# Second self attention: the values due are issued between the third and the fourth score of a step, and the maxima at its end

## The chip, the cores and the metric

The kernel runs on one core of one Trainium2 chip. The metric is the device time of one execution in microseconds, from launch to end. Engines are named as the profile names them: PE is TensorE, PEld its weight loads, ACT ScalarE, DVE VectorE, POOL GpSimd, SP the queue that issues most DMAs.

## The reference

Eight blocks follow one another on x (2 x 1024 tokens of 256): four of attention and four of feed-forward. The change is in the fourth, `_L1_ffn_ref`, whose first half is a self attention with 16 heads of width 16 over 1024 tokens:

```python
h = _layernorm(x, ln1_g, ln1_b)
qkv = h @ w_qkv + b_qkv
q, k, v = jnp.split(qkv, 3, axis=-1)
scores = jnp.einsum('bqhd,bkhd->bhqk', q, k) / np.sqrt(DK)
attn = jax.nn.softmax(scores, axis=-1)
o = jnp.einsum('bhqk,bkhd->bqhd', attn, v).reshape(B, S, D)
x = x + o @ w_o + b_o
```

A projection, a second layer norm and a mixture of experts follow. Everything outside this attention is the same in both kernels.

## The kernel before

The attention is `quad_attention` (stage `heads1`). It takes the 32 pairs of batch and head in 8 groups of four heads. A group has 16 steps: for each half of the 1024 queries (512 wide) and each of the 8 chunks of 128 keys, one step computes the transposed scores of four heads. That makes 128 steps, t = 0 to 127. Each engine has its own hand-written program, and semaphores join them.

What TensorE issues, all from these helpers:

- `score(t, r)` (L1660): one matmul, 66 x 128 weights, 512 columns, for head r. It writes `score_ps`, a ring of 3 buffers, so score number i waits until exponential number i - 3 is done. With four scores a step, the fourth waits for the first exponential of its own step.
- `share(item)` with a peak item (L1638): two bf16 matmuls on 32 rows each, from which VectorE takes part of the row maxima that a later group needs. The two of one item and the two of the next lie on four different strips of rows. They write `shared_ps`, which has two buffers: item number n waits until item n - 2 has been read.
- `value(t)` (L1669): the probabilities of step t times the values, four heads side by side in the columns of the array, 8 matmul records. It waits for the four exponentials of step t, and, for the first chunk of a half (t a multiple of 8), until ScalarE has copied the sums of the half before out of `sums_ps`, the only such buffer.
- `share` with a TURN item (L1643): once a group, the transpose of the group's maxima. `share` with a FOLD item (L1647): once a group, eight transposes of the finished sums. Both use `shared_ps` too, and both stand behind the step's peak items in the table `work_at`.

`work_at[t]` gives a step its items. Items 0 to 39 of 256 peaks are issued ahead of step 0, then two a step, so steps 0 to 107 have two peaks each and steps 108 to 127 none. TURN is in steps 12, 28, ..., 108, FOLD in steps 18, 34, ..., 114 and after the last step.

ScalarE runs the exponentials (L1705) in order. In steps 9, 17, ..., 121 it copies the sums (L1697) after the second exponential. VectorE takes the items in the order of the table: one reduction per peak item (L1721), the minus maxima (L1725), the rows of maxima (L1732, L1734), and for FOLD a reciprocal and a product (L1744, L1748). SP loads the operands of a group, and the rows of maxima after each TURN.

Before the change a step on TensorE is: four scores, the two peaks, the values of the step before, then TURN or FOLD if there is one.

Of the kernel before, what the change touches and what calls it, by code (L numbers as in the profile page):

```python
# [1528 lines left out]
QUAD = 4  # L1529


def quad_attention(nc, core, name, q_dram, k_dram, values, q_narrow, k_narrow, out):
# [39 lines left out]
    with Stage(nc, name) as st:  # L1572
# [52 lines left out]
        def _(pe):  # L1625
# [25 lines left out]
            def score(t, r):  # L1651
                g, half, c = t // PER, t % PER // BT, t % BT
                u = g % 2
                if t % PER == 0 and r == 0:
                    pe.wait_ge(loaded[u], 16 * LOADS * (g // 2 + 1))
                    pe.wait_ge(max_loaded[u], 32 * (g // 2 + 1))
                i = QUAD * t + r
                if i >= RING:
                    pe.wait_ge(exp_done, i - RING + 1)
                pe.matmul(score_ps[:, i % RING, :], k[:, u, r, c * P:(c + 1) * P],  # L1660
                          q[:, u, r, half * 512:(half + 1) * 512], start=True, stop=True).then_inc(score_done, 1)

            def value(t):
                g, c = t // PER, t % BT
                pe.wait_ge(exp_done, QUAD * (t + 1))
                if c == 0 and t:
                    pe.wait_ge(sums_copied, t // BT)
                for r, n in enumerate(heads_of(g)):
                    done = pe.matmul(sums_ps[r * SIDE:(r + 1) * SIDE, :], values[:, n, c, :],  # L1669
                                     probs[:, t % SLOTS_OF_PROBS, r, :], start=(c == 0), stop=(c == BT - 1),  # L1670
                                     tile_position=(0, r * SIDE))
                done.then_inc(value_done, 1)
# [3 lines left out]
                share(item)  # L1676
            for t in range(STEPS):
                items = work_at[t]
                for r in range(QUAD):
                    score(t, r)  # L1680
                for item in items[0:2]:
                    share(item)
                if t:
                    value(t - 1)
                for item in items[2:]:
                    share(item)
            value(STEPS - 1)
            for item in work_at[STEPS]:
# [23 lines left out]
        def _(dve):  # L1712
            def take(item):
                used = number[item]
                two = shared_ps[:, used % 2, :, :]
                dve.wait_ge(shared_done, used + 1)
                if item[0] == PEAK:
                    _, g, s, x, pair = item
                    if g >= 2 and (s, x, pair) == (0, 0, 0):
                        dve.wait_ge(minus_ready, g - 1)  # L1720
# [1328 lines left out]
```

## Time and profile before

| | |
|---|---|
| median of 3 runs | 3163.11 us (3160.62 to 3172.48) |
| the profiled execution | 3165.68 us, its span 3163.9 us |
| mean granted TensorE clock in it | 0.852 of 2.4 GHz |
| PE busy | 2409.5 us (76%) |
| DVE busy | 1544.5 us (49%) |
| ACT busy | 1126.9 us (36%) |
| the 128 steps in the trace | from 1375.8 us to about 1781.5 us |

The span goes from the first to the last instruction. The stages of the program hardly overlap, so a stage is read by itself, as a stretch of the span. PE's busy time counts a matmul from its start until its results are out; matmuls overlap, so it can be 100% while the array isn't. The granted clock is given as a share of 2.4 GHz: 1.00 is 2.4 and 0.50 is 1.2 GHz. In a timeline a row stands for one or more like instructions, with the start of the first, the time to the end of the last, and their number after the x.

### The profile page before, as it was taken

The numbers are of one execution on the slowest core, as the hardware profiler recorded it, in microseconds if no ns is written. First come the engines' busy times: TensorE is split into PE (matmuls) and PEld (weight loads), VectorE is DVE, ScalarE is ACT, GpSimd is POOL, SyncE is SP. The second block draws the span as 40 slices with busy tenths as digits, with TensorE's granted clock in tenths as the row PEclk, the third lists the DMA queues.
The fourth block names the chain that finished last, engine by engine and source line by source line (L and its number), as shares of the span: only waits on it lengthen the run. The fifth ranks groups of instructions, "written<-read, shape, count | busy, mean of one in ns | idle before, by whom it ended". The sixth has DMA issues, their size and how long they took to land. (4 is left out here: it accounts for less than half of the span.)

```text
span 3163.9 us, 38714 instructions
## 1 busy us (share of the span) xinstructions
PE 2409.5 (76%) x12273; PEld 1401.1 (44%) x12274; DVE 1544.5 (49%) x2425; ACT 1126.9 (36%) x2389; POOL 347.7 (11%) x369
## 2 busy tenths in 40 slices
PE   4959999998227587679999729996865999484487
PEld 2413333335117444323333319995333999331254
DVE  4657777763652354667786150002344000347665
ACT  3403333333103235126667424442432444233211
POOL 0010000001004201300000002221001222102211
PEclk9969999999558788759999959998786999686599
DMA  1220010100106300613342146663024666200001
GB/s 55 90 64 22 22 32 21 25 7 11 53 0 203 96 1 19 141 13 45 37 55 28 37 136 213 198 199 124 16 89 144 197 200 198 84 1 28 7 13 33
DMA packets 156570, 233.95 MB, mean 74 GB/s; under 512 B 48758, under 2 KB 110770, under 8 KB 156450
## 3 DMA queue, kind: packets, MB, share of 16 engines
q1 hardware_dynamic: 146754, 205.91, 23.8%
q0 software_dynamic: 9696, 26.49, 2.2%
q8 instruction: 69, 1.13, 0.2%
q14 instruction: 51, 0.42, 0.0%
HBM read 186.56 MB, written 38.86 MB: 71 GB/s over the span
## 5 line engine op out<-in xcount | busy, mean ns | idle before, releaser
L1721 DVE TENSOR_REDUCE heads_part_max<-heads_shared_ps 128x2 f32<-128x1024 f32 x256 | 300.0, 1220 | 90.1 <-PE heads_shared_ps L1638 90.1
L2759 PE MATMUL experts_up_ps<-experts_rowT,experts_w 128*128 128x128 f32 x2864 | 341.0, 277 | 0.0
L1705 ACT ACTIVATE heads_probs<-heads_score_ps 128x512 f32<-128x512 f32 x512 | 266.4, 602 | 191.0 <-PE heads_score_ps L1660 191.0
L2759 PEld LDWEIGHTS experts_up_ps<-experts_rowT,experts_w 128*128 128x128 f32 x2864 | 333.0, 194 | 0.2
L1408 ACT ACTIVATE heads_probs<-heads_score_ps 128x512 f32<-128x512 f32 (+1 forms) x288 | 171.9, 598 | 382.1 <-PE heads_score_ps L1332 380.3
L2909 DVE TENSOR_TENSOR experts_y<-experts_down_ps,experts_b_now 128x256 f32<-128x256 f32 x78 | 33.1, 425 | 555.6 <-PE experts_down_ps L2769 555.6
L1332 PE MATMUL heads_score_ps<-heads_q,heads_k 128*128 128x512 f32 (+1 forms) x576 | 291.6, 616 | 0.3 <-DVE heads_minus_max L1420 0.3
L2819 ACT ACTIVATE experts_hT<-experts_up_ps,experts_b_now 128x128 f32<-128x128 f32 x624 | 222.6, 368 | 46.5 <-PE experts_up_ps L2759 9.8
L1660 PE MATMUL heads_score_ps<-heads_q,heads_k 66*128 66x512 f32 x512 | 198.0, 474 | 29.5 <-ACT heads_probs L1705 25.3
L1420 DVE TENSOR_REDUCE heads_minus_max<-heads_shared_ps 128x1 f32<-128x1101 f32 x120 | 155.9, 1299 | 113.5 <-PE heads_shared_ps L1307 113.4
L2769 PE MATMUL experts_down_ps<-moe_w,experts_hT 128*128 x808 | 184.4, 379 | 0.0
L1660 PEld LDWEIGHTS heads_score_ps<-heads_q,heads_k 66*128 66x128 f32 x512 | 92.2, 201 | 198.4 <-ACT heads_probs L1705 163.5
L2769 PEld LDWEIGHTS experts_down_ps<-moe_w,experts_hT 128*128 128x128 f32 x808 | 148.9, 190 | 17.8
L1344 PE MATMUL heads_sums_ps<-heads_probs,heads_head_values 128*64 128x512 f32 (+1 forms) x576 | 154.6, 605 | 0.0
L1669 PE MATMUL heads_sums_ps<-heads_probs,self_values 128*32 128x512 f32 x1024 | 146.8, 647 | 4.1 <-ACT heads_sums L1697 4.1
L2708 POOL DMA_INDIRECT y_dram<-experts_y,experts_index x101 | 99.4, 985 | 454.3 <-DVE experts_y L2909 410.4
L2769 PE MATMUL experts_down_ps<-l1f_w,experts_hT 128*128 x624 | 141.0, 379 | 0.0
L1458 DVE TENSOR_TENSOR heads_weights<-heads_probs,heads_weights 128x1024 f32<-128x1024 f32 (+1 forms) x112 | 136.2, 1216 | 6.4 <-ACT heads_probs L1408 5.2
L1332 PEld LDWEIGHTS heads_score_ps<-heads_q,heads_k 128*128 128x128 f32 (+1 forms) x576 | 92.1, 187 | 92.4 <-issue 71.5
L2800 ACT ACTIVATE experts_rowT<-experts_rowT_ps 128x256 f32<-128x256 f32 x62 | 23.8, 384 | 296.4 <-PE experts_rowT_ps L2749 296.3
L2769 PEld LDWEIGHTS experts_down_ps<-l1f_w,experts_hT 128*128 128x128 f32 x624 | 115.7, 190 | 14.1
L1307 PE MATMUL heads_shared_ps<-heads_k_peak,heads_q_peak 128*128 128x512 bf16 x360 | 80.9, 335 | 40.7 <-DVE heads_k_peak L1480 26.0
(556 smaller groups left out, 3370.3 us busy)
## 6 DMA issues: line engine op xcount, KB each, us to landing
experts_w<-in_L_ffn_W SPq DMA_DIRECT2D x39, 1024.0 KB, 5.2
experts_w<-in_L_ffn_w SPq DMA_DIRECT2D x39, 1024.0 KB, 5.1
heads_q<-l_queries SPq DMA_DIRECT2D x48, 256.0 KB, 12.1
experts_w<-in_L_ffn_W SPq DMA_DIRECT2D x23, 512.0 KB, 3.9
core_xT<-y_dram SPq DMA_DIRECT2D x20, 512.0 KB, 4.7
experts_b_now<-in_L_ffn_b SPq DMA_DIRECT2D x78, 128.0 KB, 2.9
heads_k<-l_keys SPq DMA_DIRECT2D x32, 256.0 KB, 14.0
l1f_w<-in_L_ffn_W SPq DMA_DIRECT2D x8, 1024.0 KB, 11.9
```

The costliest lines, as they stand in the source:

```text
L1332: pe.matmul(score_ps[0:rows, i % RING, :], k[:, u, c * P:c * P + rows], q[:, u, x:x + spec.unit], start=True, stop=True).then_inc(score_do ...
L1344: done = pe.matmul(sums_ps[x * SIDE:(x + 1) * SIDE, part * spec.unit:(part + 1) * spec.unit], head_values[0:rows, u, c, :], probs[0:rows, ...
L1408: act.activation(probs[0:rows, slot(u, i), :], score_ps[0:rows, i % RING, :], ACT.Exp, scale=spec.scale).then_inc(exp_done, 1)
L1420: dve.tensor_reduce(minus_max[:, u, s:s + 1], src[:, 0:KEYS], AX.X, ALU.max, negate=True).then_inc(shared_read, 1)
L1458: dve.tensor_tensor(total, chunk_probs(u, c)[0:rows, :], chunk_probs(u, 0) if c == 1 else total, ALU.add).then_inc(added, 1)
L1660: pe.matmul(score_ps[:, i % RING, :], k[:, u, r, c * P:(c + 1) * P], q[:, u, r, half * 512:(half + 1) * 512], start=True, stop=True).then_ ...
L1669: done = pe.matmul(sums_ps[r * SIDE:(r + 1) * SIDE, :], values[:, n, c, :], probs[:, t % SLOTS_OF_PROBS, r, :], start=(c == 0), stop=(c == ...
L1705: act.activation(probs[:, t % SLOTS_OF_PROBS, r, :], score_ps[:, i % RING, :], ACT.Exp, scale=SC).then_inc(exp_done, 1)
L1721: dve.tensor_reduce(part_max[:, g % 2, 2 * pair:2 * pair + 2, s, x], two, AX.X, ALU.max).then_inc(shared_read, 1)
L2759: done = pe.matmul(up_ps[:, f % 4, 0:SLOT], w1_sb[:, u, c, f * P:(f + 1) * P], rowT[:, u % 2, c, :], start=(c == 0), stop=(c == DC - 1))
L2769: done = pe.matmul(down_ps[:, u % 2, 0:D], hT[:, u % 2, f, :], second.sb[:, bass.ds(e, 1), f, :].rearrange("p o d -> p (o d)"), start=(f = ...
L2819: act.activation(hT[:, u % 2, f, :], up_ps[:, f % 4, 0:SLOT], func, bias=bias).then_inc(act_done, 1)
```

## The change

In every step TensorE now issues three scores, then the values of the step before, then the fourth score, and then all items of the step: the two peaks, and TURN or FOLD behind them. No instruction is added or removed, and no other engine's program changes.

```diff
@@ -1676,13 +1676,12 @@
                 share(item)
             for t in range(STEPS):
                 items = work_at[t]
-                for r in range(QUAD):
+                for r in range(QUAD - 1):
                     score(t, r)
-                for item in items[0:2]:
-                    share(item)
                 if t:
                     value(t - 1)
-                for item in items[2:]:
+                score(t, QUAD - 1)
+                for item in items:
                     share(item)
             value(STEPS - 1)
             for item in work_at[STEPS]:
```

On PE around the first TURN (steps 12 and 13; L1660 scores, L1638 peaks, L1669 values, L1643 the TURN transpose), before:

```order
L1660 MATMUL heads_score_ps<-heads_q,heads_k 128x512 x4
L1638 MATMUL heads_shared_ps<-self_k_narrow,self_q_narrow 128x512 x4
L1669 MATMUL heads_sums_ps<-heads_probs,self_values 32x512 x4
L1643 MATMUL heads_shared_ps<-core_ident,heads_minus_max 32x128
L1660 MATMUL heads_score_ps<-heads_q,heads_k 128x512 x4
```

and now:

```order
L1660 MATMUL heads_score_ps<-heads_q,heads_k 128x512 x3
L1669 MATMUL heads_sums_ps<-heads_probs,self_values 32x512 x4
L1660 MATMUL heads_score_ps<-heads_q,heads_k 128x512
L1638 MATMUL heads_shared_ps<-self_k_narrow,self_q_narrow 128x512 x4
L1643 MATMUL heads_shared_ps<-core_ident,heads_minus_max 32x128
L1660 MATMUL heads_score_ps<-heads_q,heads_k 128x512 x3
```

A step has gone from three blocks of matmuls to four, and the TURN transpose, which had the values between itself and the peaks, now stands right behind the peaks.

On PE around the first FOLD (steps 18 and 19; L1647 are the eight transposes of the sums), before:

```order
L1660 MATMUL heads_score_ps<-heads_q,heads_k 128x512 x4
L1638 MATMUL heads_shared_ps<-self_k_narrow,self_q_narrow 128x512 x4
L1669 MATMUL heads_sums_ps<-heads_probs,self_values 32x512 x4
L1647 MATMUL heads_shared_ps<-core_ident,heads_sums 128x128 x8
L1660 MATMUL heads_score_ps<-heads_q,heads_k 128x512 x4
```

and now:

```order
L1669 MATMUL heads_sums_ps<-heads_probs,self_values 32x512 x4
L1660 MATMUL heads_score_ps<-heads_q,heads_k 128x512
L1638 MATMUL heads_shared_ps<-self_k_narrow,self_q_narrow 128x512 x4
L1647 MATMUL heads_shared_ps<-core_ident,heads_sums 128x128 x8
L1660 MATMUL heads_score_ps<-heads_q,heads_k 128x512 x3
```

FOLD too has lost the values that stood between it and the peaks.

## Rows read from the trace of the kernel before

**Rows 1.** Windows: us, busy of PE, PEld, DVE, ACT, POOL, PEclk, DMA share, GB/s.

```profile
1376.00:1435.00 59.00, 59.00 (x203) 18.95 (x204) 31.02 (x28) 27.50 (x53) 0.00 (x0) 0.50 0.00 1
1435.00:1727.00 292.00, 264.65 (x1575) 93.73 (x1574) 232.88 (x219) 202.10 (x392) 0.00 (x0) 1.00 0.38 45
```

**Rows 2.** Line L1660, all scores: ns min/median/max, first and last start.

```profile
L1660 PE MATMUL heads_score_ps<-heads_q,heads_k x512: 389/494/796, 1375.8 to 1780.1; 66*128 66x512 f32 x171
```

**Rows 3.** Timeline (start us, us, ...), PE, step 6, clock 0.50.

```profile
1400.90 1.08 PE L1669 MATMUL heads_sums_ps<-heads_probs,self_values 128*32 128x512 f32 x4
1401.91 0.80 PE L1660 MATMUL heads_score_ps<-heads_q,heads_k 66*128 66x512 f32 x1
...
1402.93 0.63 PE L1660 MATMUL heads_score_ps<-heads_q,heads_k 66*128 66x512 f32 x1
1403.39 0.79 PE L1660 MATMUL heads_score_ps<-heads_q,heads_k 66*128 66x512 f32 x1
1404.12 0.61 PE L1638 MATMUL heads_shared_ps<-self_k_narrow,self_q_narrow 32*128 32x512 bf16 x4
1404.66 1.94 PE L1669 MATMUL heads_sums_ps<-heads_probs,self_values 128*32 128x512 f32 x8
1406.53 0.80 PE L1660 MATMUL heads_score_ps<-heads_q,heads_k 66*128 66x512 f32 x1
```

**Rows 4.** Timeline, step 0 into step 1, clock 0.50: no values between.

```profile
1377.96 0.61 PE L1638 MATMUL heads_shared_ps<-self_k_narrow,self_q_narrow 32*128 32x512 bf16 x4
...
1378.51 1.22 PE L1660 MATMUL heads_score_ps<-heads_q,heads_k 66*128 66x512 f32 x2
1378.61 1.23 DVE L1721 TENSOR_REDUCE heads_part_max<-heads_shared_ps 128x2 f32<-128x1024 f32 x1 [5.84 <-PE heads_shared_ps L1638]
```

**Rows 5.** Timeline, PE and DVE, step 53, clock 1.00.

```profile
1558.08 0.96 PE L1660 MATMUL heads_score_ps<-heads_q,heads_k 66*128 66x512 f32 x3
...
1559.26 0.49 PE L1660 MATMUL heads_score_ps<-heads_q,heads_k 66*128 66x512 f32 x1 [0.23 <-ACT heads_probs L1705]
...
1559.69 0.40 PE L1638 MATMUL heads_shared_ps<-self_k_narrow,self_q_narrow 32*128 32x512 bf16 x4
...
1560.01 1.07 PE L1669 MATMUL heads_sums_ps<-heads_probs,self_values 128*32 128x512 f32 x8
...
1560.12 2.36 DVE L1721 TENSOR_REDUCE heads_part_max<-heads_shared_ps 128x2 f32<-128x1024 f32 x2 [0.58 <-PE heads_shared_ps L1638]
...
1561.01 0.50 PE L1660 MATMUL heads_score_ps<-heads_q,heads_k 66*128 66x512 f32 x1
```

**Rows 6.** Timeline, PE, step 116 (no peaks), clock 1.00.

```profile
1750.68 0.50 PE L1660 MATMUL heads_score_ps<-heads_q,heads_k 66*128 66x512 f32 x1 [0.22 <-ACT heads_probs L1705]
1751.11 1.07 PE L1669 MATMUL heads_sums_ps<-heads_probs,self_values 128*32 128x512 f32 x8
```

**Rows 7.** Timeline, step 25, in which ScalarE copies the sums.

```profile
1471.34 0.96 PE L1660 MATMUL heads_score_ps<-heads_q,heads_k 66*128 66x512 f32 x3
...
1472.85 0.60 ACT L1697 ACTIVATE heads_sums<-heads_sums_ps 128x512 f32<-128x512 f32 x1
...
1473.60 1.06 PE L1669 MATMUL heads_sums_ps<-heads_probs,self_values 128*32 128x512 f32 x8 [0.25 <-ACT heads_sums L1697]
```

**Rows 8.** Timeline, PE and DVE, step 50, which has FOLD.

```profile
1550.09 2.36 DVE L1721 TENSOR_REDUCE heads_part_max<-heads_shared_ps 128x2 f32<-128x1024 f32 x2 [0.89 <-PE heads_shared_ps L1638]
...
1551.37 1.09 PE L1647 MATMUL heads_shared_ps<-core_ident,heads_sums 128*128 128x128 f32 x8 [0.32 <-DVE heads_part_max L1721]
...
1552.22 0.95 PE L1660 MATMUL heads_score_ps<-heads_q,heads_k 66*128 66x512 f32 x3
```

**Rows 9.** Timeline, PE, steps 12 and 13, round the rise of the clock.

```profile
1432.38 1.94 PE L1669 MATMUL heads_sums_ps<-heads_probs,self_values 128*32 128x512 f32 x8
1434.25 0.40 PE L1643 MATMUL heads_shared_ps<-core_ident,heads_minus_max 128*32 128x128 f32 x1
1434.30 1.96 PE L1660 MATMUL heads_score_ps<-heads_q,heads_k 66*128 66x512 f32 x4
```

## Prediction

> **What bounds the kernel now.** I read the windows of the stage first, then the groups of line L1660, then timelines of single steps at either clock. The stage takes from the first score at 1375.8 us to the last at 1780.1 us [rows 2] and 1.43 more to the end of step 127 (score to values 0.43 [rows 6], values to the next score 1.00 [rows 5]): 405.7 us for 128 steps. It has two parts. Until about 1435 us TensorE runs at 0.50, that is 1.2 GHz, though its row is busy 59.00 of 59.00 us; from there it runs at 1.00, 2.4 GHz [rows 1]. The reader is to see that a full PE row did not bring the clock up for 13 steps, and that a step takes 4.62 us before (1401.91 to 1406.53 [rows 3]) and 2.93 after (1558.08 to 1561.01 [rows 5]).
>
> At 2.4 GHz the step is a loop on PE with one stall: the fourth score waits for the first exponential (0.23 us idle, and 1.18 after the first score [rows 5]). ScalarE itself has slack. At 1.2 GHz there is no stall to remove: the fourth score is 0.46 behind the third, and the scores' own pace is close to that [rows 3].
>
> **The change, step by step.** No instruction comes or goes. What changes is how often TensorE goes from one kind of matmul to another: three times a step before (scores, peaks, values), four times now (scores, values, score, peaks). I cost each block from start to start.
>
> At 1.2 GHz: first to third score 1.02 (1402.93 - 1401.91 [rows 3]); score to values has no row at this clock. At 2.4 GHz it is 0.43 [rows 6], and score to peaks is 0.43 too (1559.69 - 1559.26 [rows 5]), so I take score to peaks at 1.2 GHz, 0.73 (1404.12 - 1403.39 [rows 3]). Its bounds: 0.46, a score behind a score, and 1.01, a score behind the second half of the values (1401.91 - 1400.90 [rows 3]). Values to score is 1.87 (1406.53 - 1404.66), score to peaks 0.73 [rows 3], peaks to score 0.55 (1378.51 - 1377.96 [rows 4]). Sum 1.02 + 0.73 + 1.87 + 0.73 + 0.55 = 4.90, against 4.62: each slow step gets **0.28 us longer**.
>
> These gaps are the price of changing kinds: 0.73 where a score behind a score takes 0.46. The Trainium skill, in TensorE: Matmul & The Clock Gate, Step-by-step: what each phase is for, has TensorE load the next weights while the present matmul still runs, into a background buffer. By that alone score to values would be 0.46, and my total some 29 us lower (107 x 0.27); the trace has the gap.
>
> At 2.4 GHz: 0.57 (the three scores' 0.96 [rows 5] less the shortest single one, 0.39 [rows 2]) + 0.43 + 1.00 + 0.43 + 0.32 (peaks to values, 1560.01 - 1559.69 [rows 5], taken for peaks to score, since the two are 0.54 and 0.55 at the other clock [rows 3, 4]) = 2.75. The fourth score no longer waits, its slot being free long before 2.00. Next in line is VectorE: peaks to reduction 0.43 and two reductions 2.36 [rows 5], release 0.05 (first reduction, half of 2.36 with its overlap, 1.23 alone in [rows 4], to FOLD at 1551.37 [rows 8]): 2.84. The second peak item waits for that in every other step, so 2.80 on average. **Gain 0.13** in an ordinary step.
>
> Three kinds of step lose at either clock, because what hid a wait is gone:
> - Copy steps (15). The values wait for ScalarE's copy, and ScalarE's order is as before, so they start 2.26 after the first score in both kernels (1473.60 - 1471.34 [rows 7]). Behind them stood only the next step, 1.00; now stand 1.00 + 0.43 + 0.32. **Loss 0.75** against before.
> - TURN and FOLD steps. Both need VectorE to have read the step's first peak item: 0.43 + 1.23 + 0.05 = 1.70 after the peaks. The peaks were at 1.61 (1559.69 - 1558.08 [rows 5]) with the values in that wait; now they are at 2.43 and nothing is in it. **Loss 0.82** each.
>
> SP's loads and the rows of maxima have over three steps of slack and cost nothing; if that cover went, the 4.2 us of a load of maxima would show at a group's start.
>
> **When does the clock rise?** This decides the size. Before, step after step of 4.62 us left the clock at 0.50. It rose only after step 12, where something was different: TURN came right behind the values and the next scores 0.05 behind it (1434.25, 1434.30 [rows 9]), so the usual changeover was filled. In the changed kernel the same products are spread over 4.90 us instead of 4.62, with one more changeover. And TURN and FOLD now follow a wait, from the peaks 0.65 (1378.61 - 1377.96 [rows 4]) + 1.23 + 0.05 = 1.92 us, in which TensorE has nothing. If 4.62 us steps did not raise the clock, I expect that 4.90 us steps won't, nor TURN or FOLD behind a wait. So the likeliest course is that **the clock stays at 0.50 for the stage**. All at 1.2 GHz:
> - step 0: 2.7 (1378.51 less 1375.8 [rows 2, 4]); steps 1 to 107: 107 x 4.90 = 524.3
> - steps 108 to 127, without peaks: 1.02 + 0.73 + 1.87 + 0.46 = 4.08, x 20 = 81.6
> - TURN, 6 with peaks: peaks at 4.35, + 1.92 + 0.05 = 6.32, 1.42 over 4.90: 8.5
> - FOLD, 6 with peaks: 4.35 + 1.92 + 1.70 (0.85 [rows 8], doubled with the clock) = 7.97, 3.07 over: 18.4; the one in step 114: 1.7
> - copies: values at 2.56, not 1.75, as the first score takes 0.80, not 0.50 [rows 3, 5]: 0.81 x 15 = 12.2
>
> Together 649.4, less 405.7: 243.7, and 2 for the last values and FOLD at half clock: +246 on the profiled execution's 3165.68, so **3411 us**. The median of the runs shown, 3163.11, is 2.6 lower. The bounds of score to values (0.46 to 1.01, 127 times) move it by -34 and +36; a rise in the last 20 steps would give back up to 29 (4.08 less 2.6 each), which lies within the lower one. Own range 3377 to 3440.
>
> **Rivals.**
> 1. *The clock rises at step 12 or so, as before.* For it: it did so with a step only 6% shorter, and the rise may hang on something else than the filled changeover. Then 12 slow steps cost 3.4, the copy and TURN in them 2.2; at 2.4 GHz 72 ordinary steps give 9.4, 12 copies cost 9.0, 5 TURN and 6 FOLD 9.0, the last 20 steps 0.9. Sum +15: 3181. The gain is there and is eaten by the three kinds of step.
> 2. *It rises late*, behind some TURN or FOLD. Each slow step costs 2.1 over a fast one: at step 66 it gives 3181 + 53 x 2.1 = 3292; the span of this case is 3190 to 3370.
> 3. *The other side: the clock rises early*, in the first steps, because the values now come between scores and fill the fourth score's wait. It decides from step 1 on: 13 steps fall from 58.5 us to 38, and the losses of rival 1 beyond them are 9.5: 3155, not slower. Against it: 59.00 us of full PE row at 0.50 [rows 1], and denser steps than the new ones in them. The Trainium skill, same page, What's actually happening, says that activity releases the throttle, so a full row should have brought 2.4 GHz soon; by that the result is this rival's. The trace disagrees for 13 steps.
>
> That the order isn't what the words say can be left out: the instruction order shows it.
>
> **The numbers.** Clock stays down 0.66; as before 0.17; late 0.10; early 0.05; the rest, 0.02, an error of mine in the fast step's size that makes it faster. A measurement of this kernel tells about 0.5% (16 us) from no change, so the bounds are 3147 and 3179. Faster: 0.03 (half of early, a little of the rest). Same: 0.10 (the rest of early, and under half of "as before", which lies at the edge). Slower: 0.87. The stay-down case holds too little alone, so the range goes down through the late rise to the middle of "as before": 3175 to 3440.
>
> **What would show it.** In the changed profile: the windows from 1376 on with PEclk 0.50 for some 650 us of stage, steps of 4.90 us with score to values near 0.73 and peaks to score near 0.55; ScalarE waiting longer for scores; the values in copy steps 2.5 us behind the first score; TURN and FOLD 1.9 us behind the peaks. Wrong would be: PEclk 1.00 from about 1435 us with steps of 2.75 and 2.84 (rival 1), or steps under 2.7 us at 2.4 GHz, which would mean that VectorE's loop doesn't bind.

## The result, and the profile after

The changed kernel takes 3375.2 us (median of 4 runs, 3371.76 to 3381.08). Before, with one more run beside it, the median is 3161.86 (4 runs, 3142.36 to 3172.48). The ratio is **1.068, 95% interval 1.063 to 1.074**: slower by 213 us. The forecast was 3411, 246 slower.

The profiled execution of after took 3381.08 us, its span is 3379.1 and its mean granted clock 0.781 (before 3165.68, 3163.9 and 0.852). The difference to explain is 215.4 us. The first score stands at 1375.9 us in after and at 1375.8 in before [rows 2], so everything before the stage takes the same time. The scores of after, in the groups of their line:

```profile
L1660 PE MATMUL heads_score_ps<-heads_q,heads_k x512: 390/628/797, 1375.9 to 1986.6; 66*128 66x512 f32 x171
```

First to last score takes 610.7 us, against 404.3 [rows 2]: **206.4 of the 215.4 us lie in the stage**. The median score takes 628 ns instead of 494, while the shortest stays where it was (390 and 389). That is one cause acting on most scores, and the windows name it (us, busy of PE, PEld, DVE, ACT, POOL, then PEclk, DMA share, GB/s):

```profile
1376.00:1470.00 94.00, 89.56 (x306) 28.72 (x306) 45.48 (x41) 42.15 (x78) 0.00 (x0) 0.50 0.19 23
1474.00:1487.00 13.00, 13.00 (x80) 4.64 (x76) 11.33 (x10) 10.56 (x20) 0.00 (x0) 1.00 0.01 1
1490.00:1940.00 450.00, 426.93 (x1454) 135.38 (x1454) 205.23 (x195) 198.64 (x368) 0.00 (x0) 0.50 0.20 24
1945.00:1960.00 15.00, 13.40 (x68) 4.80 (x64) 0.00 (x0) 11.75 (x23) 0.00 (x0) 1.00 0.00 0
```

The clock is at 1.2 GHz for the whole stage but for two stretches, from 1473.3 and from 1944.3 us, of 17.1 us each. Before it rose at 1435.6 and stayed [rows 1]. TensorE's row is 95% busy in the 450 us at the lower clock, so it isn't idleness that a reader would see on the page. DVE and ACT, 80% and 69% busy in before's fast part (232.88 and 202.10 of 292.00 us [rows 1]), are 46% and 44% busy: they wait for a slower TensorE.

I compared the starts of each step's first score in the two traces, and sorted the 127 differences (they add up to 204.1; the other 2.3 lie within the last step) by the clock at the start of the step in both:

| steps | count | before, us | after, us | difference |
|---|---|---|---|---|
| at 0.50 in both | 14 | 61.7 | 66.4 | +4.7 |
| at 1.00 before, 0.50 after | 101 | 307.1 | 504.4 | +197.2 |
| of these ordinary, with peaks | 66 | 193.5 | 310.4 | +116.8 |
| at 1.00 in both | 12 | 34.2 | 36.4 | +2.2 |

Of the +197.2, the copy steps with peaks take 26.8 (11), FOLD steps 21.3 (6) and TURN steps 13.9 (5); the rest are steps without peaks. What the new order costs without the clock is small. What the clock costs is the result.

An ordinary slow step of after (step 5, timeline of PE), for comparison with [rows 3]:

```profile
1402.21 1.65 PE L1660 MATMUL heads_score_ps<-heads_q,heads_k 66*128 66x512 f32 x3
1403.79 1.94 PE L1669 MATMUL heads_sums_ps<-heads_probs,self_values 128*32 128x512 f32 x8
1405.65 0.80 PE L1660 MATMUL heads_score_ps<-heads_q,heads_k 66*128 66x512 f32 x1
1406.38 0.61 PE L1638 MATMUL heads_shared_ps<-self_k_narrow,self_q_narrow 32*128 32x512 bf16 x4
1406.92 1.65 PE L1660 MATMUL heads_score_ps<-heads_q,heads_k 66*128 66x512 f32 x3
```

The step is 4.71 us (1406.92 - 1402.21). Its blocks from start to start are 1.58 for the three scores up to the values, 1.86, 0.73 and 0.54. With 1.02 from first to third score [rows 3], score to values is 0.56.

How the clock rises and falls in after. First the rise at 1473.3 us, behind the first FOLD (step 18 into 19, timeline of PE; in brackets the idle time ahead and what ended it):

```profile
1466.31 0.61 PE L1638 MATMUL heads_shared_ps<-self_k_narrow,self_q_narrow 32*128 32x512 bf16 x4
1468.24 1.97 PE L1647 MATMUL heads_shared_ps<-core_ident,heads_sums 128*128 128x128 f32 x8 [1.32 <-DVE heads_part_max L1720]
1469.86 1.63 PE L1660 MATMUL heads_score_ps<-heads_q,heads_k 66*128 66x512 f32 x3
1471.41 1.94 PE L1669 MATMUL heads_sums_ps<-heads_probs,self_values 128*32 128x512 f32 x8
1473.28 0.50 PE L1660 MATMUL heads_score_ps<-heads_q,heads_k 66*128 66x512 f32 x1
```

FOLD starts 1.93 behind the peaks, as forecast (1.92), after 1.32 us of idle. The fourth score, 0.80 long in the slow step, is 0.50 at 1473.28: the clock has risen. Then the fall at 1490.3, six fast steps later, in step 25, in which ScalarE copies the sums (timeline):

```profile
1487.84 0.96 PE L1660 MATMUL heads_score_ps<-heads_q,heads_k 66*128 66x512 f32 x3
...
1489.34 0.60 ACT L1696 ACTIVATE heads_sums<-heads_sums_ps 128x512 f32<-128x512 f32 x1
...
1490.09 1.75 PE L1669 MATMUL heads_sums_ps<-heads_probs,self_values 128*32 128x512 f32 x8 [1.29 <-ACT heads_sums L1696]
...
1491.78 0.80 PE L1660 MATMUL heads_score_ps<-heads_q,heads_k 66*128 66x512 f32 x1
```

The values wait 1.29 us for the copy, where the same step of before waited 0.25 [rows 7], because then the fourth score and the peaks stood in that time. The clock falls at 1490.3, 0.2 us behind the start of the values. Summed over the stage, the idle time ahead of the values (L1669) of after that ends with ScalarE's copy, in us and times:

```profile
  ACT heads_sums L1696: 13.9, 15
```

Before, it was 4.1 us. Ahead of TURN and of FOLD, TensorE now stands still for 1.32 us in each of the six steps that have it together with peaks. The stops came as predicted. What I had not thought of is that a stop of a good microsecond might take the clock down.

### The profile page after: what moved, and what is told of

Same layout as the page of the kernel before. It is cut to its first block and busy times, and to the rows that moved or that the text cites. A ratio compares the mean times of both kernels' runs of the same rounds, so it can differ in the third digit from the quotient of the medians.

```text
span 3379.1 us, 38714 instructions
## 1 busy us (share of the span) xinstructions
PE 2625.7 (78%) x12273; PEld 1461.0 (43%) x12274; DVE 1545.0 (46%) x2425; ACT 1123.7 (33%) x2389; POOL 348.2 (10%) x369
## 5 line engine op out<-in xcount | busy, mean ns | idle before, releaser
L1704 ACT ACTIVATE heads_probs<-heads_score_ps 128x512 f32<-128x512 f32 x512 | 278.1, 598 | 385.7 <-PE heads_score_ps L1660 385.7
L1660 PE MATMUL heads_score_ps<-heads_q,heads_k 66*128 66x512 f32 x512 | 298.6, 686 | 5.5 <-DMA heads_q<-heads_max_rows 4.2
L1660 PEld LDWEIGHTS heads_score_ps<-heads_q,heads_k 66*128 66x128 f32 x512 | 138.3, 299 | 269.7 <-issue 235.9
L1669 PE MATMUL heads_sums_ps<-heads_probs,self_values 128*32 128x512 f32 x1024 | 237.8, 1020 | 14.6 <-ACT heads_sums L1696 13.9
L2818 ACT ACTIVATE experts_hT<-experts_up_ps,experts_b_now 128x128 f32<-128x128 f32 x624 | 207.3, 368 | 82.2 <-PE experts_up_ps L2758 65.3
L1638 PE MATMUL heads_shared_ps<-self_k_narrow,self_q_narrow 32*128 32x512 bf16 x512 | 89.0, 592 | 31.5 <-DVE heads_part_max L1720 21.0
```

Source lines behind the costliest of these rows:

```text
L1704: act.activation(probs[:, t % SLOTS_OF_PROBS, r, :], score_ps[:, i % RING, :], ACT.Exp, scale=SC).then_inc(exp_done, 1)
L2818: act.activation(hT[:, u % 2, f, :], up_ps[:, f % 4, 0:SLOT], func, bias=bias).then_inc(act_done, 1)
```

## The experiments

The questions are two. **What raises the clock?** My theory on record: the changeover that TURN filled in before, that is, an order in which TURN stands directly behind the values. The rival: the density of the slow steps (4.62 us raise it by themselves, with some delay, and 4.71 do not). **What takes it down?** The theory formed from the trace above: the new stops of TensorE in copy, TURN and FOLD steps. The rival: the four-block order can't hold it. In what follows "stage" is first to last score, rises and falls are read from each trace's granted clock, and medians stand beside runs of the kernel before on the same chip.

### Take the copy's stop away

ScalarE copies the sums at the end of the step before, so that the values of the next do not wait.

```diff
-                    if r == 1 and t > 1 and t % BT == 1:
+                    if r == QUAD - 1 and t and t % BT == 0:
                         copy(t // BT - 1)
```

> The changed order, but ScalarE copies the sums one step earlier, behind the fourth exponential of steps 8, 16, ..., 120, so that the values of steps 9, 17, ... find the copy done. My theory: the clock is lost in this order to two things, ordinary slow steps of 4.71 us that do not raise it, and the 1.3 us in which TensorE stands still in a copy step, which takes it back down. Then here the clock rises behind a FOLD (step 18, or a later one) and stays at 1.00 to the end of the stage: 3150 to 3200 us if at step 18, about 30 us more for each group later. Rival (the fall in step 25 has another cause, for example that steps of 2.74 us do not hold the clock): it falls again and the time stays within 20 us of 3375.

Measured: 3267.9 us (two runs, 3252.1 and 3283.7), ratio 1.033 (1.020 to 1.045), stage 492.6. The clock rose in step 19 behind the first FOLD, as in after, and now passed every copy step. It held for 123 us, until TURN in step 60. The timeline of PE there:

```profile
1587.32 0.59 PE L1638 MATMUL heads_shared_ps<-self_k_narrow,self_q_narrow 32*128 32x512 bf16 x4
1589.03 0.28 PE L1643 MATMUL heads_shared_ps<-core_ident,heads_minus_max 128*32 128x128 f32 x1 [1.13 <-DVE heads_part_max L1720]
1589.07 0.95 PE L1660 MATMUL heads_score_ps<-heads_q,heads_k 66*128 66x512 f32 x3
1589.96 1.78 PE L1669 MATMUL heads_sums_ps<-heads_probs,self_values 128*32 128x512 f32 x8
1591.67 0.80 PE L1660 MATMUL heads_score_ps<-heads_q,heads_k 66*128 66x512 f32 x1
```

TURN waited 1.13 us for VectorE, the values' 1.78 is neither fast (1.07) nor slow (1.94), and the score after them is slow: the fall, at 1590.2. It rose again behind the FOLD of step 82, fell at TURN in step 92, and rose at the FOLD of step 114. But two earlier TURNs (28 and 44) and two FOLDs (34 and 50), with stops of the same size, had left it up. So a stop is where it falls, but not each stop makes it fall. Against the 3375.2 of the changed kernel the edit is worth some 107 us, from two runs that lie 32 us apart.

### Take the stops of TURN and FOLD away

TURN and FOLD of a step are issued in the next step, between values and fourth score, when VectorE has long read the peaks.

```diff
+            late = []
             for t in range(STEPS):
...
                     value(t - 1)
+                for item in late:
+                    share(item)
                 score(t, QUAD - 1)
                 for item in items:
-                    share(item)
+                    if item[0] == PEAK:
+                        share(item)
+                late = [item for item in items if item[0] != PEAK]
...
```

> The changed order, but TURN and FOLD are held back by a step and issued between the values and the fourth score, so nothing waits for VectorE. The copy waits stay. My theory: saved for certain are the waits at 1.2 GHz, 6 x 1.4 for TURN and 6 x 1.4 for FOLD, 17 us, so 3358; since TURN and FOLD again stand right behind the values, the clock may rise at more of them and fall at the next copy, at most 5 to 7 fast steps of each 8: 3230 to 3358. Rival (waits at TURN and FOLD are the main cause, copies are not): the clock stays up from step 13 on, 3150 to 3170.

Measured: 3223.8 us (two runs), ratio 1.019 (1.013 to 1.023), stage 466.0. It rose in step 19 once more. Now the copy steps are where it falls. In step 57 (timeline of PE):

```profile
1585.30 1.22 PE L1669 MATMUL heads_sums_ps<-heads_probs,self_values 128*32 128x512 f32 x8 [1.29 <-ACT heads_sums L1701]
1586.46 0.80 PE L1660 MATMUL heads_score_ps<-heads_q,heads_k 66*128 66x512 f32 x1
```

A second fall came in the step behind copy step 73, a third in copy step 113. Eight other copy steps, in which the values waited the same 1.29 us, left the clock up. Each half of the stops removed gives part of the time back, and the falls move to the half that is left.

### Take both away

> The changed order with both remedies: copies one step earlier, TURN and FOLD a step later between the values and the fourth score. No stop over 0.3 us of TensorE is left. My theory: where the clock has risen (at the latest behind the FOLD of step 18, issued in step 19) it does not fall again in the stage; then 19 slow steps of 4.71, 89 of 2.74 on average, TURN and FOLD 11 more, 20 steps of 2.61: stage 398 us against 404, total 3150 to 3165. Rival (in this order the clock also falls in ordinary steps): falls outside of TURN, FOLD and copy steps, over 3180.

With both edits the kernel takes 3155.2 us (10 runs), ratio 0.998 (0.996 to 1.001), stage 400.1. The windows:

```profile
1371.00:1462.00 91.00, 91.00 (x309) 27.75 (x308) 45.57 (x41) 43.74 (x81) 0.00 (x0) 0.50 0.20 23
1466.00:1770.00 304.00, 295.52 (x1696) 108.09 (x1698) 218.74 (x208) 236.45 (x444) 0.00 (x0) 1.00 0.30 36
```

It rose once, in step 19 at FOLD, and stayed up for 314 us, through every TURN, FOLD and copy. **The same four blocks a step, without the stops, hold the clock to the end**, so the order by itself does not lose it; the rival falls. "Without the stops" means those over a microsecond: six of 0.50 to 0.63 us are left behind FOLD, where peaks wait for VectorE, and the clock passed all six. The two edits together recover the 213 us that the change cost. The row of the first 91 us is the other half of the story: 91.00 of 91.00 us busy, and the clock stays at 0.50 through steps 0 to 18, until FOLD comes.

### The order of before, with TURN and FOLD at the peaks

This undoes the moved score and keeps TURN and FOLD where the change has put them, directly behind the peaks. By my theory the clock then needs FOLD to rise, since nothing fills the changeover behind the values.

```diff
-                for r in range(QUAD - 1):
+                for r in range(QUAD):
                     score(t, r)
-                if t:
-                    value(t - 1)
-                score(t, QUAD - 1)
                 for item in items:
                     share(item)
+                if t:
+                    value(t - 1)
```

> The order of before, with one part of the change alone: TURN and FOLD stand directly behind the peaks and ahead of the values. Steps stay at 4.62 and 2.93 us. My theory: the clock no longer rises at the TURN of step 12; it rises at the FOLD of step 18 (plus 10 us), or a group later (plus 37) or never (plus 180), and where it has risen it stays, for a copy step stands still only 0.25 us. Rival (the place of TURN has nothing to do with the rise at step 12, it is the time since the fall or the length of the step): it rises within two steps of before, 3160 to 3172.

Measured: 3214.0 us (two runs), ratio 1.016 (1.011 to 1.020), stage 454.1. The timeline of PE in step 10, where the clock rose for the first time:

```profile
1418.05 0.61 PE L1638 MATMUL heads_shared_ps<-self_k_narrow,self_q_narrow 32*128 32x512 bf16 x4
1418.59 1.94 PE L1669 MATMUL heads_sums_ps<-heads_probs,self_values 128*32 128x512 f32 x8
1420.46 1.98 PE L1660 MATMUL heads_score_ps<-heads_q,heads_k 66*128 66x512 f32 x4
1422.38 0.39 PE L1638 MATMUL heads_shared_ps<-self_k_narrow,self_q_narrow 32*128 32x512 bf16 x4
```

The peaks take 0.61 in one step and 0.39 in the next. TURN comes two steps later, and ScalarE's copy in step 9 makes TensorE wait for nothing: **an ordinary step of 4.62 us raised the clock**. It did so three times more, in steps 70, 80 and 96. That ends my theory of the rise. The four falls all stand at a TURN; six more TURNs and FOLDs at the higher clock waited the same 1.32 us and left it up, the first in step 12. My expectation that it stays where it has risen failed with them. The fall in step 44:

```profile
1531.57 0.40 PE L1638 MATMUL heads_shared_ps<-self_k_narrow,self_q_narrow 32*128 32x512 bf16 x4
1533.28 0.28 PE L1643 MATMUL heads_shared_ps<-core_ident,heads_minus_max 128*32 128x128 f32 x1 [1.32 <-DVE heads_part_max L1719]
1533.49 1.25 PE L1669 MATMUL heads_sums_ps<-heads_probs,self_values 128*32 128x512 f32 x8
1534.67 2.27 PE L1660 MATMUL heads_score_ps<-heads_q,heads_k 66*128 66x512 f32 x4
```

So stops take the clock down in the order of before as well, and that order gets it back within 4 to 10 steps, which is why it loses 52 us in the median and not 213.

### Start the stage at the higher clock

Sixteen matmuls whose results nobody reads are issued ahead of step 0, in the changed kernel and in the kernel before. What they add to the computation is not part of the output.

```diff
+            for i in range(16):
+                pe.matmul(score_ps[:, i % RING, :], q_narrow[:, 0, 0:P], k_narrow[:, 0, 0, 0:512],
+                          start=True, stop=True)
             for t in range(STEPS):
```

> The changed order, with 16 further matmuls of 512 columns between the first TURN and step 0, whose results nobody reads; they fill a wait of 4.2 us of TensorE for the maxima and cost about 3 us. They are to bring the clock to 1.00 before step 0. My theory: steps 1 to 8 take 2.74 us, and the copy step 9 takes the clock down again, so about 9 x 2 us are saved less 3: near 3360. Rival (a copy step does not take it down; the order was only never raised): 1.00 to the end of the stage, near 3140.

In the changed kernel: 3362.2 us (two runs), ratio 1.062 (1.058 to 1.067), stage 596.8. Its windows:

```profile
1377.00:1414.00 37.00, 34.40 (x199) 12.08 (x197) 29.75 (x27) 28.43 (x53) 0.00 (x0) 1.00 0.00 1
1417.00:1929.00 512.00, 485.86 (x1656) 156.13 (x1656) 234.41 (x220) 225.93 (x418) 0.00 (x0) 0.50 0.22 26
```

The clock was up from 1374.2, passed the first copy step, and fell at 1415.2, 1.1 us behind the TURN of step 12, which had waited 1.12 us. It did not come back until 1930.6. A fast start is worth some 13 us to the changed kernel: what it lacks is not the start, it is that it cannot keep the clock.

> The order of before with the same 16 unread matmuls ahead of step 0. My theory (the price of this stage is its clock): PEclk is 1.00 from step 0 on, steps 1 to 12 take 2.93 instead of 4.62 us, less 2 us for the fill: about 18 us faster than before, 3145. It has no stop over 0.3 us in a copy or TURN step, so it stays up. Rival (a step of this order too loses the clock within some steps): within 5 us of before or slower.

In the kernel before: 3155.2 us (10 runs), ratio 0.999 (0.997 to 1.001), no measurable gain and 10 us behind the 3145 that I had expected. The timeline of PE in step 1 shows why:

```profile
1377.67 0.46 PE L1638 MATMUL heads_shared_ps<-self_k_narrow,self_q_narrow 32*128 32x512 bf16 x2 [0.50 <-DVE heads_part_max L1724]
1378.05 1.93 PE L1669 MATMUL heads_sums_ps<-heads_probs,self_values 128*32 128x512 f32 x8
```

The peaks wait for VectorE, 0.50 us, and the values behind them run their full slow length. The clock fell at 1377.9. Four slow steps followed, and step 5, an ordinary one, brought it back at 1398.3 for good. The kernel before with early copy and the same sixteen matmuls, which comes further down, makes the same wait in step 1 and keeps its clock, so a wait of this size does not always bring the fall:

```profile
1379.69 0.39 PE L1638 MATMUL heads_shared_ps<-self_k_narrow,self_q_narrow 32*128 32x512 bf16 x2 [0.50 <-DVE heads_part_max L1724]
1380.01 1.07 PE L1669 MATMUL heads_sums_ps<-heads_probs,self_values 128*32 128x512 f32 x8
```

### Three blocks a step, with the stops removed

To see whether it is the order or its stops that keeps a slow step from raising the clock, I put the fourth score back with the other three and kept the early copy and late TURN and FOLD (the diff is against the kernel with both). A step is then scores, values, peaks: three changes of kind as before, though in another order.

```diff
                 for r in range(QUAD - 1):
                     score(t, r)
+                score(t, QUAD - 1)
                 if t:
                     value(t - 1)
                 for item in late:
                     share(item)
-                score(t, QUAD - 1)
```

> Both remedies as in the kernel before the last, but the fourth score stands with the other three, so a step is four scores, values, peaks: three blocks, not four, 4.63 us at 1.2 GHz and 2.93 at 2.4. It tells whether the lone score is what keeps ordinary slow steps from raising the clock. My theory: it is (its step holds the same products in 4.71 us): here the clock rises in an ordinary step by step 13, as in the order of before, stage 395 to 402, total 3155 to 3163. Rival (the rise needs the old place of the peaks ahead of the values): no rise before the FOLD issued in step 19, stage 410 or more.

Measured: 3205.7 us (4 runs, spread from 3178.0 to 3230.5), ratio 1.013 (1.006 to 1.020), stage 423.0 in the profiled run of 3191.2. The windows of its first 110 us:

```profile
1377.00:1398.00 21.00, 20.98 (x72) 6.93 (x72) 9.43 (x8) 10.38 (x20) 0.00 (x0) 0.50 0.00 1
1400.00:1440.00 40.00, 36.73 (x218) 12.41 (x217) 32.01 (x30) 28.91 (x57) 0.00 (x0) 1.00 0.23 29
1448.00:1485.00 37.00, 37.00 (x132) 11.44 (x128) 19.02 (x17) 17.34 (x34) 0.00 (x0) 0.50 0.02 3
```

The half that I had been sure of failed: the median is some 46 us over the expected time. In this order FOLD is followed at once by peaks, of which the second pair waits 0.86 us for VectorE, which is still dividing the sums. At three of the six places with peaks the clock fell 1.6 to 2.1 us behind that wait (in steps 20, 52 and 100); the others, in steps 35, 67 and 83, left it up. The half that was in doubt held: the slow steps are 4.62 us long, and **all four rises are in ordinary steps** (5, 56 and 104, and 29 ahead of its transpose).

### More work between the changes of kind

If what counts is how much TensorE streams between two changes of kind, then a four-block step with more scores in it should rise as the 4.62 us step does. Here both stop-removing edits are in, and in steps 0 to 17 the fourth score is computed three times over; only the last result is read.

```diff
+            def again(t):
...
+                for _ in range(2):
+                    pe.matmul(score_ps[:, i % RING, :], k[:, u, QUAD - 1, c * P:(c + 1) * P],
+                              q[:, u, QUAD - 1, half * 512:(half + 1) * 512], start=True, stop=True)
...
+                if t < 18:
+                    again(t)
                 score(t, QUAD - 1)
```

> The changed order with early copy and late TURN and FOLD, but without the fill; in steps 0 to 17 TensorE computes the fourth score three times over into the same buffer, and only the last is read. A slow step gets longer (4.71 + 0.85 = 5.56 us), with the same changes of kind and more streaming. My theory (ordinary slow steps of the changed order are too thinly filled for the clock to rise; what they lack is streaming between the changes of kind): the clock rises in an ordinary step before 18, as steps of 4.62 us did in the orders with three blocks. Rival (it is the number of changes of kind, or the step's length, that keeps it down): no rise before the transposes issued in step 19, or of TURN in step 13, and a stage longer than the same kernel without the repeats by about 16 us, near 3171.

Measured: 3176.6 us (8 runs), ratio 1.005 (1.003 to 1.006), stage 414.6. Its windows:

```profile
1376.00:1470.00 94.00, 94.00 (x307) 33.32 (x306) 40.86 (x37) 38.51 (x72) 0.00 (x0) 0.50 0.09 12
1482.00:1780.00 298.00, 289.54 (x1663) 106.18 (x1661) 220.80 (x210) 230.55 (x432) 0.00 (x0) 1.00 0.31 37
```

The slow steps are 5.57 us, without a gap, with more scores per change of kind than in any order here, and the clock stayed at 0.50 until FOLD in step 19, as without the extra scores; it rose at 1481.2, 0.4 us behind the start of the transposes. That explanation falls too: more scores in a four-block step did not raise the clock.

### Both stops removed, and a fast start

> As the last one, with the 16 unread matmuls ahead of step 0. My theory: PEclk 1.00 through the stage, 107 steps of 2.74, 20 of 2.61, TURN and FOLD 11 more: stage 363 us against 404, total about 3125, which is 1.2% under before and the fastest of all; it would show that the order itself is worth 0.19 us a step once the clock is held. Rival (the order is no gain in itself): not under the order of before with the same fill.

> The order of before, with the 16 unread matmuls and the early copy, but TURN and FOLD where they were, since in this order they cost no stop over 0.3 us. It is the fairest partner of the fastest kernel so far (the changed order with early copy, late TURN and FOLD, and the same 16 matmuls, 3127.6 us), and gives what the order by itself is worth. My theory: with the clock up a step is 2.93 us here and 2.74 there, 95 such steps make 18 us, so this kernel gives 3140 to 3150, a little more where the clock is lost for some steps at the start as before. Rival (the order is worth nothing, the gain came from fill and early copy): 3125 to 3132.

Early copy, late TURN and FOLD and the sixteen unread matmuls give **3127.6 us (4 runs, 3124.94 to 3131.18), ratio 0.991 (0.988 to 0.993)**, the fastest of all, ahead of both kernels. The kernel before with the early copy and the same sixteen matmuls gives 3153.3 (10 runs), ratio 0.997 (0.994 to 0.999). In their profiled runs both have the clock at 1.00 for the whole stage, which is the comparison of the two orders that the change itself doesn't allow. The 10 runs of the second spread from 3134.2 to 3166.4 us with mean granted clocks from 0.866 to 0.853, so not all of them can be taken to have held it; the stages below are of one run each. The stage of the new order and of the old, windows of the one and then of the other:

```profile
1376.00:1727.00 351.00, 342.37 (x1974) 125.64 (x1974) 266.31 (x251) 272.56 (x510) 0.00 (x0) 1.00 0.32 37
```

```profile
1376.00:1750.00 374.00, 340.50 (x1988) 120.51 (x1987) 266.75 (x251) 265.43 (x516) 0.00 (x0) 1.00 0.29 35
```

The stage is 361.9 us in the first and 380.4 in the second: **the new order is worth 18.5 us** once nothing stops it and the clock is held. The same PE work (342 and 340 us) is done in less time, its row being 98% busy instead of 91%. A fast step of the first (timeline of PE), against [rows 5]:

```profile
1431.65 0.96 PE L1660 MATMUL heads_score_ps<-heads_q,heads_k 66*128 66x512 f32 x3
1432.54 1.06 PE L1669 MATMUL heads_sums_ps<-heads_probs,self_values 128*32 128x512 f32 x8
1433.54 0.49 PE L1660 MATMUL heads_score_ps<-heads_q,heads_k 66*128 66x512 f32 x1
1433.96 0.40 PE L1638 MATMUL heads_shared_ps<-self_k_narrow,self_q_narrow 32*128 32x512 bf16 x4
1434.29 0.97 PE L1660 MATMUL heads_score_ps<-heads_q,heads_k 66*128 66x512 f32 x3
```

The fourth score no longer waits for the exponential (0.23 us idle in [rows 5], none here), and the step is 2.64 us; the next one is 2.84. So the idea of the change does what it is meant to do.

### What the traces say together

| kernel | median, us | stage, us | first rise | falls |
|---|---|---|---|---|
| before | 3161.9 | 404.3 | step 13, 1.3 us behind TURN | none |
| after | 3375.2 | 610.7 | 19, behind FOLD | copy, copy |
| early copy | 3267.9 | 492.6 | 19, behind FOLD | TURN, TURN |
| late TURN and FOLD | 3223.8 | 466.0 | 19, behind FOLD | copy, behind copy, copy |
| both | 3155.2 | 400.1 | 19, at FOLD | none |
| order of before, TURN at peaks | 3214.0 | 454.1 | 10, ordinary | TURN, four times |
| three blocks, both | 3205.7 | 423.0 | 5, ordinary | behind FOLD, three times |

In orders with slow steps of 4.62 us, nine of eleven rises stand in ordinary steps, in some 60 such steps. In the orders with four blocks (4.71 us, and 5.57 in the kernel with more scores, which the table leaves out together with the changed kernel with the fast start, whose counts are in here) none does in about 240. All eleven rises come during FOLD's or TURN's transposes or within 3.2 us of their end; ten of the eleven are at a FOLD, out of 24 FOLDs at the lower clock. These counts come from one profiled execution of each kernel. The clock never fell in the middle of an unbroken row: every fall is at a stop of TensorE or in the step behind one. Over all twelve traces, a fall came with 13 of the 32 stops of 1.06 to 1.32 us that met the higher clock in the stage, with 3 of the 6 of 0.86 us, and with 1 of the 32 of 0.50 to 0.63 us. The falls are shown to hang on the stops by removing them (no fall in 314 us); that each stop needs something more to bring the fall about is shown only by the many that were passed, and what it is stays open.

The times of the other executions bear on the rise as well. 43 runs of the kernel before that ran beside these experiments took 3145.81 to 3171.79 us with mean granted clocks of 0.862 to 0.850, the slower ones mostly at the lower clock. An ordinary step costs 1.69 us more when it is slow (4.62 against 2.93), so these 26 us would be some 15 slow steps more or fewer, an estimate. The one trace of that kernel, with its rise in step 13, is then one of a spread, and no property of that step. The traces of the other runs were not kept, so where their clocks rose is not shown.

## Why the prediction was right or wrong

**Right: direction and cause.** Slower had 0.87, the course with the clock down 0.66, and that is what happened; the time, 3375.2, is 36 below the forecast, in the range and just under the case's own range of 3377 to 3440. (Its stated terms of -34 and +36 give 3377 to 3447, and the sums given as 1.70 and 1.92 are 1.71 and 1.93; neither matters here.)

**The slow step.** Forecast 1.02 + 0.73 + 1.87 + 0.73 + 0.55 = 4.90, measured 1.02 + 0.56 + 1.86 + 0.73 + 0.54 = 4.71. Four terms hold to 0.01. The second, *score to values*, was mis-sized: there was no row for it, and I took score to peaks, 0.73. What the rows show is that a score which stands alone between other kinds, or is the fourth of a row, holds the next kind some 0.17 longer than the last of a row of three does. The next kind is not the reason: in the kernel with three blocks the fourth score of the row is followed by values, and they too start 0.72 behind it. Before, the fourth score followed its third at 0.46, but its own length was 0.79 [rows 3], and I had not asked why one score should be 0.63 long and the next 0.79. No run shows why. The rule of the Trainium skill that I weighed there (TensorE: Matmul & The Clock Gate, Step-by-step: what each phase is for) would have given 0.46; the measured 0.56 lies nearer to it than to my 0.73, while the lone fourth score, at 0.73 to the peaks, does not follow it. It lies inside my bounds of 0.46 to 1.01, and for 107 steps the 0.19 is worth 20 us.

**Three special steps.** TURN came out at 6.15 (forecast 6.32), that is 1.44 over an ordinary step (1.42); FOLD at 7.72 (7.97), 3.01 over (3.07). The copy step is 5.69, 0.98 over (0.81). The two stops behind VectorE, 1.92 us from the peaks, were 1.93 in the trace.

**The last 20 steps** are 4.07 (4.08), which is right by two errors that cancel. Without peaks the fourth score of a step and the three of the next stand in one row of four (steps 110 to 112 of after, timeline of PE):

```profile
1922.90 2.28 PE L1660 MATMUL heads_score_ps<-heads_q,heads_k 66*128 66x512 f32 x4
1925.11 1.94 PE L1669 MATMUL heads_sums_ps<-heads_probs,self_values 128*32 128x512 f32 x8
1926.97 2.28 PE L1660 MATMUL heads_score_ps<-heads_q,heads_k 66*128 66x512 f32 x4
```

The 2.21 us up to the values are 0.59 from the fourth score to the next step's first (forecast 0.46), 0.89 from there to the third (1.02), and 0.73 to the values, as forecast. Values to score is 1.86.

**The clock "stays at 0.50 for the stage".** It nearly did. Two stretches of 17.1 us were at 1.00: some six steps behind the first FOLD at 2.74 on average instead of 4.71 give 11 us (the clock changes within the first and the last of them), and six without peaks at 2.61 instead of 4.07 give 9. From the forecast difference of 243.7: less 20 for the mis-sized term, less 20 for these, plus 2 for the copies is 206; the trace has 206.4 up to the last score. The remaining 9 us of the 215.4 lie behind the stage, where I had 2: from the last score to the experts' rise of the clock 125.0 us instead of 123.1, and 1267.5 instead of 1260.7 from there to the end, which I followed no further.

**The reason was wrong, though the outcome was right.** The step of the prediction that failed is: "It rose only after step 12, where something was different: TURN came right behind the values ... so the usual changeover was filled." With TURN at the peaks the clock rose in step 10 without any TURN, and in eight more ordinary steps in three kernels. What I had read from one place was a coincidence, or one of several ways; in this part the forecast was right by luck. The sentence after it failed as well: "nor TURN or FOLD behind a wait". FOLD behind a wait of 1.32 us is exactly where the changed kernel's clock rose. What was right in it is the comparison itself: "If 4.62 us steps did not raise the clock, I expect that 4.90 us steps won't". 4.71 us steps of four blocks never did, although 4.62 us steps of three blocks did.

**What I missed: the clock can also fall.** I costed the new stops (0.75, 0.82 and 0.82 us) as stops, and in rival 1 let the clock stay up from step 12 through 23 of them. The run with the fast start tests that rival directly, more kindly than its own terms: it fell within 41 us, and the kernel took 3362 instead of 3181. Rival 1 was not possible as I put it, and its chance of 0.17 was too much. Rival 3 needs a rise in the first steps: no kernel with 4.71 us steps had it unaided. Rival 2 is nearest to what came, with the rise given back after 17 us each time.

**Fast steps.** Forecast 2.75 and 2.84, bound by TensorE and by VectorE's loop in turn; measured 2.64 and 2.84, 2.74 on average. The gain of an ordinary step against 2.93 is 0.19, not 0.13. The term that was off is score to values again: the three scores up to the values take 0.89 (1431.65 to 1432.54), not 0.57 + 0.43. It is in the trace, and over the stage with the clock held it gives the 18.5 us.

**The Trainium skill** (same page, What's actually happening) says that activity releases the throttle. After the first FOLD's stretch the changed kernel kept its PE row busy 426.93 of 450.00 us at 0.50, and the kernel without the long stops kept it busy 91.00 of 91.00: the traces of both disagree with the rule, as [rows 1] did for 59 us. Another section of that page, A second HAM failure mode: psum-queue depth-cycling, says that a kernel which goes idle briefly and often between groups of matmuls can make the clock go back and forth. With that the falls at stops of 1.06 to 1.32 us agree, though 19 of the 32 such stops were passed.

**What stays open.** Why ordinary steps of 4.71 us in four blocks do not raise the clock and those of 4.62 us in three blocks do, after 4 to 10 of them. Length alone does not decide it, nor more scores per block. Nor does the number of changes of kind. In the last 20 steps there are only two of them, a row of four scores and the values, yet 30 such slow steps of 4.07 us in four kernels raised no clock by themselves. With late TURN and FOLD the stage ends at 0.50, with a row nearly as full (windows):

```profile
1784.00:1842.00 58.00, 57.24 (x174) 19.35 (x173) 1.05 (x2) 29.05 (x57) 0.00 (x0) 0.50 0.00 0
```

Those steps have no peaks, so they differ from the others in more than the number of changes. Among the steps with peaks, four changes against three fits all traces, and so do the place of the lone score and other things that go with it; I tried no order that separates them. Why the clock rose at 10 of the FOLDs and not at the other 14 is open too.

## What to carry to other kernels

Read the granted clock of a stage before costing an edit in it, and cost the edit at both levels: here the reorder gained 0.19 us a step at one level and cost 101 steps some 2 us each by losing it. A wait of about 1 us that costs little as time may cost the clock, so when blocks of TensorE are reordered, look at what stood in the shadow of each rare wait (copies, transposes) and move its producer earlier in the same edit. If one place in a trace seems to explain a rise of the clock, find a second place before building on it.

## What the runs showed that I had not expected

- The clock fell at stops of 1.06 to 1.32 us, at three of 0.86 and at one of 0.50 us, inside a row otherwise nearly full, and many stops of the same size left it up: in the kernel with late TURN and FOLD 8 of 11 copy steps passed.
- A slow stretch is stable. The changed kernel ran 454 us at 1.2 GHz with its TensorE 95% busy, and 515 us after it had been started at 2.4.
- Sixteen unread matmuls ahead of the stage brought the clock up, at a price too small to be seen, and with the long stops gone it held for the whole stage: 3155.2 without them, 3127.6 with them.
- A score that stands alone between other kinds, or is the fourth of a row, costs 0.17 us more at 1.2 GHz than the last of three (0.73 against 0.56 to the next kind).
